# Batch 1's first projections in the ramp, GpSimd as the engine that normalises, three places for rows of q and k, and a new order of the work on every engine

## The reference, cut to what matters

```python
x = layernorm(x + attn(x))        # 32 heads on 8 key/value heads of 8 features, softmax over 256 keys
x = layernorm(x + wkv(x, ctx))    # scan over time: y = (sum of exp(..k) * v) / (sum of exp(..k)), decay w, bonus u
x = layernorm(x + ffn(x))
# ffn: h = square(relu(x @ up_w)) (256 -> 1024); h @ down_w + (x @ expert_weight) * (sum of the top 2 of 8 gate logits)
#      and inside it y is normalised with ln_gamma and ln_beta before the residual is added
def layernorm(x): return (x - mean(x)) / sqrt(var(x) + 1e-5)
```

## Time and profile before

| | |
|---|---|
| median of 3 runs | 216.61 us (215.62 to 217.32) |
| profiled execution: time, span | 216.79 us, 215.0 us |
| TensorE busy | 199.7 us (93%) |
| VectorE busy | 163.1 us (76%) |
| ScalarE busy | 150.9 us (70%) |
| GpSimd busy | 129.6 us (60%) |
| first attention unit, first exponential unit | 13.29 us, 24.80 us |
| exponential unit 64, end of the last unit | 83.65 us, about 169.6 us |
| last matmul | 208.0 us |

### The profile page before, as it was taken

One profiled execution on the slowest core, in us unless ns is written; L12 is line 12 of the kernel. 1 busy time (PEld: TensorE's weight loads), 2 busy tenths in 40 slices (PEclk: granted clock), 3 DMA queues, 4 the chain that ended last, 5 costly groups with the idle time before them and its releaser, 6 DMA issues.

```text
span 215.0 us, 4364 instructions
## 1 busy us (share of the span) xinstructions
PE 199.7 (93%) x1295; PEld 111.7 (52%) x1295; DVE 163.1 (76%) x392; ACT 150.9 (70%) x334; POOL 129.6 (60%) x256
## 2 busy tenths in 40 slices
PE   8889999979999899999999999999999998799970
PEld 3533543433433334575465445664655487698950
DVE  3469778778999899998979899976754837956274
ACT  2310477867899789989799879998967984763520
POOL 8995164753465724567476786867495493177622
PEclk9999999999999999999999999999999999999996
DMA  3145227943116602131000000010000000000001
GB/s 122 43 117 170 70 56 226 255 127 108 27 44 203 218 2 64 49 90 36 19 9 7 2 0 9 2 33 25 2 6 0 3 24 26 2 5 0 24 24 49
DMA packets 14759, 12.35 MB, mean 57 GB/s; under 512 B 3856, under 2 KB 12688, under 8 KB 14480
## 3 DMA queue, kind: packets, MB, share of 16 engines
q1 hardware_dynamic: 14064, 11.72, 19.0%
q10 hardware_dynamic: 672, 0.36, 0.6%
HBM read 6.57 MB, written 1.05 MB: 35 GB/s over the span
## 4 chain that ended last, share of the span: by engine, by line
PE 71%; DMA 8%; DVE 7%; ACT 6%; issue 5%; ACTq 1%; POOL 1%; POOLq 0%; DVEq 0%
PE ps_b L781 10%; PE ps_heads L629 10%; PE ps_exp L613 10%; PE ps_b L764 9%; DMA q_rows<-max_t 7%; PE ps_max L600 6%; PE ps_exp L635 4%; PE ps_exp L764 3%; PE ps_b L747 3%; PE ps_a L722 3%; PE ps_a L676 2%; ACT probs L812 2%; PE ps_a L665 2%; DVE maxima L1180 2%; PE ps_a L585 2%
## 5 line engine op out<-in xcount | busy, mean ns | idle before, releaser
L1180 DVE TENSOR_REDUCE maxima<-ps_max 128x2 f32<-128x512 f32 x128 | 85.0, 684 | 10.6 <-PE ps_max L600 9.7
L812 ACT ACTIVATE probs<-ps_exp 128x512 f32<-128x512 f32 x128 | 73.6, 599 | 14.6 <-PE ps_exp L613 14.1
L613 PE MATMUL ps_exp<-q_rows,k_rows 64*128 64x512 bf16 x128 | 46.2, 385 | 3.8 <-ACT probs L812 1.7
L600 PE MATMUL ps_max<-k_rows,q_rows 64*128 64x256 bf16 x256 | 47.4, 274 | 0.7 <-DMA q_rows<-q_parts 0.6
L613 PEld LDWEIGHTS ps_exp<-q_rows,k_rows 64*128 64x128 bf16 x128 | 11.4, 93 | 45.0 <-ACT probs L812 25.9
L629 PE MATMUL ps_heads<-probs,v_cols 128*32 128x512 f32 x256 | 33.9, 604 | 0.0
L781 PE MATMUL ps_b<-down_sb,inner_t 128*128 128x256 f32 x112 | 29.4, 388 | 0.7 <-ACT relu_t L943 0.7
L764 PE MATMUL ps_b<-x_t,up_sb 128*128 128x128 f32 x192 | 27.1, 285 | 1.1 <-DVE h L1367 1.1
L1061 POOL TENSOR_TENSOR rstd<-var_eps,minus_half 128x1 f32<-128x1 f32 x32 | 19.6, 611 | 11.7 <-DVE var_eps L1154 11.7
L764 PEld LDWEIGHTS ps_b<-x_t,up_sb 128*128 128x128 f32 x192 | 23.2, 191 | 6.0 <-issue 4.0
L781 PEld LDWEIGHTS ps_b<-down_sb,inner_t 128*128 128x128 f32 x112 | 19.4, 190 | 4.3 <-issue 1.5
(11 more groups left out here) (129 smaller groups left out, 345.2 us busy)
## 6 DMA issues: line engine op xcount, KB each, us to landing
q_rows<-q_parts SPq DMA_DIRECT2D x46, 64.0 KB, 2.1
x_t<-in_x_cols SPq DMA_DIRECT2D x4, 256.0 KB, 3.3
x_in<-in_x SPq DMA_DIRECT2D x4, 256.0 KB, 4.5
ctx_t<-in_ctx_cols SPq DMA_DIRECT2D x4, 256.0 KB, 3.0
up_sb<-in_up_w SPq DMA_DIRECT2D x1, 1024.0 KB, 6.1
down_sb<-in_down_w SPq DMA_DIRECT2D x1, 1024.0 KB, 6.1
out_y<-y_out SPq DMA_DIRECT2D x8, 128.0 KB, 1.7
post_sb<-in_w_post SPq DMA_DIRECT2D x1, 906.0 KB, 5.5
```

The costliest lines, as they stand in the source:

```text
L600: last = nc.tensor.matmul(ps_max[n % 2][:, r, :], q_rows[b][at:at + HALF, g, REP * jj + 2 * half + r, h * P:h * P + P], k_rows[b][at:at + ...
L613: nc.tensor.matmul(ps_exp[n % 2][:, :], k_rows[b][at:at + HALF, JH * g + jj, kt * P:kt * P + P], q_rows[b][at:at + HALF, g, REP * jj:REP * ...
L812: nc.scalar.activation(probs[n % 8][:, :], ps_exp[n % 2][:, :], ACT.Exp, scale=SCALE).then_inc(s_exp, 1)
L1180: nc.vector.tensor_reduce(maxima[s % 2][:, g, j // JH, 0, at:at + 2], ps_max[n % 2][:, :, :], AX, ALU.max, negate=True).then_inc(s_max, 1)
```

## The change

1. **Ramp.** Batch 1's x is loaded at the very start. Its k and first q projection (AT 2315 and 2379 before, inside the first units) go to 1618 and 1839, before the first unit. Three idle matmuls follow each of k(1), v(0) and q1(0); the 16 that waited for the rows before the first unit are gone.
2. **Copies of batch 0.** The three copies of k's middle and low part go from ScalarE's queue to GpSimd's, and ScalarE's issues all three copies of group 0's later q parts. Group 0's parts of maxima are made on GpSimd and its `max_t` is evacuated by ScalarE (both VectorE before), v(0) is evacuated by ScalarE, and VectorE fills batch 1's `q_rows`.
3. **Norms.** For p < 6 GpSimd adds epsilon, takes the power and applies mean and rstd (L997 in the new kernel). The negated mean, the offset and ScalarE's part are gone, as is VectorE's addition.
4. **Three places for rows.** `q_rows` and `k_rows` have three tiles instead of four (ROT): batch 3 takes batch 0's, waits until its exponentials are made, and copies zeros over two rows. `probs` has 12 buffers instead of 8.
5. **Order.** Nearly all numbers of AT are new.

```diff
-        "k": (1456, 2315, 2440, 3400),
+        "k": (1474, 1618, 2440, 3368),
-        "q0": (1503, 2379, 2792, 3624),
+        "q0": (1520, 1839, 2762, 3720),
...
+    ROT = 3
+    NPROBS = 12
...
             sp.dma_start(qk_sb[:, KV_COLS:], w_qk[:, KV_COLS:]).then_inc(s_wq, 16)
+            sp.dma_start(flat(x_t[1][:, :, :]), x_cols[1]).then_inc(s_xt[1], 16)
...
+            def rows_free(b):
+                sp.wait_ge(s_ones, ROT + (b >= 2))
+                if b == 1:
+                    sp.wait_ge(s_q1_zero, 1)
+                if b >= ROT:
+                    sp.wait_ge(s_exp, UNITS * TT * (b - ROT + 1))
...
+                                if b >= ROT and qp == 0:
+
+                                    sp.dma_start(row_block(q_rows[b % ROT][:, g], len(BLOCKS)),
+                                                 row_block(q_rows[1][:, g], len(BLOCKS) + 1)).then_inc(s_rows[b][g], 16)
...
-                    if n == 0:
-
-                        for done, value, n_idle in ((s_q2[0], 1, ROW_FILL), (s_q3[0], 1, 6 * ROW_FILL),
-                                                    (s_krows[0], 16 * len(BLOCKS), ROW_FILL)):
-                            pe.wait_ge(done, value)
-                            for k in range(n_idle):
-                                idle_matmul(ident_bf)
...
+                        if b == 1:
+                            for k in range(FILL):
+                                idle_matmul(ident_bf)
...
-                for kp, done in ((1, s_k2), (2, s_k3)):
-                    if AT[f"kc{kp}"][0] == tick:
-                        act.wait_ge(s_ones, 1)
-                        act.wait_ge(done, 1)
-                        k_row_copies(act, 0, kp)
...
+                    if b == 0 and AT["vb"][0] == tick:
+                        act.wait_ge(s_const, 1)
+                        a_filled(act, ("v", 0))
+                        nc.scalar.activation(
+                            heads_of(v_cols[0])[:, :, :, 0:HD],
+                            ps_a[:, 0:TT * KVD].rearrange("p (x j d) -> p x j d", j=GS, d=HD), ACT.Copy).then_inc(s_a_read, 1)
...
+            gp.wait_ge(s_ones, 1)
+            for kp, done in ((1, s_k2), (2, s_k3)):
+                gp.wait_ge(done, 1)
+                k_row_copies(gp, 0, kp, s_krows_pool)
+            gp.memset(q_rows[2][:], 0.0).then_inc(s_ones, 1)
...
+            def normalise(k, p, src, dst, done):
+                gp.wait_ge(s_rstd[k], p + 1)
+                for i in CHUNKS[p][1]:
+                    last = gp.tensor_scalar(dst[:, i, :], src[:, i, :], mean_var[k][:, i, 0:1], rstd[k][:, i:i + 1],
+                                            ALU.subtract, ALU.mult)
+                last.then_inc(done, 1)
...
                             if p < WIDE:
-                                gp.tensor_scalar(neg_mean[k][:, ti], mean_var[k][:, ti, 0], -1.0, None,
-                                                 ALU.mult).then_inc(s_negmean[k], 1)
+                                gp.tensor_scalar(var_eps[k][:, ti], mean_var[k][:, ti, 1], EPS, None,
+                                                 ALU.add).then_inc(s_pool, 1)
+                                npool[0] += 1
+                                gp.wait_ge(s_pool, npool[0])
                             gp.tensor_tensor(rstd[k][:, ti], var_eps[k][:, ti], minus_half[:, ti],
                                              ALU.pow).then_inc(s_rstd[k], 1)
...
+            nc.vector.memset(q_rows[1][:], 0.0).then_inc(s_q1_zero, 1)
```

More of the change, by code:

```diff
@@ new lines, in decoder_layer @@
+        "qc02": (1762, 2656, 3604, 4853),
+        "qc10": (1997, 2958, 3467, 4355),
+        "qc11": (1938, 2853, 3658, 4953),
+        "qc12": (1903, 2941, 3639, 4940),
+        "load": (2173, 2207, 2241, 2578, 2835, 3158, 3326, 3367, 3620, 3709, 4718, 4872, 4979),
[17 rows of a table added]
+        "att": (3181, 3821, 4176, 4700, 5200, 5704, 6125, 6799),
+        "att_e": (3167, 3839, 4217, 4703, 5183, 5661, 6110, 6826),
+        "xbo": (3008, 3038, 3451, 4485, 4864, 5098, 5717, 5824),
[30 rows of a table added]
+        "unit": (4213, 4790, 5355, 5581, 6121, 6242, 6990, 7629),
@@ L275, in decoder_layer @@
         max_t = sb("max_t", [P, NSET, P], bf16)
-        probs = [sb(f"probs{i}", [P, REP * P]) for i in range(8)]
+        probs = [sb(f"probs{i}", [P, REP * P]) for i in range(NPROBS)]
         heads_t = [sb(f"heads_t{i}", [P, REP * P]) for i in range(2)]
@@ L310, in decoder_layer @@
         rstd = [sb(f"rstd{i}", [P, TT]) for i in range(4)]
-        neg_mean = [sb(f"neg_mean{i}", [P, TT]) for i in range(4)]
-        offset = [sb(f"offset{i}", [P, TT]) for i in range(4)]
         ps_max = [ps(f"ps_max{i}", [P, 2, T]) for i in range(2)]
@@ L505, in load @@
             def load(j):
-                tiles = ((x_t[1], x_cols[1], s_xt[1]), (x_in[0], x[0], s_x[0]), (ctx_t[0], ctx_cols[0], s_ctx[0]),
+                tiles = ((x_in[0], x[0], s_x[0]), (ctx_t[0], ctx_cols[0], s_ctx[0]),
                          (x_t[2], x_cols[2], s_xt[2]), (post_sb, w_post, s_w_post), (up_sb, up_w, s_up),
@@ L678, in _ @@
                             last.then_inc(s_q0 if b == 0 else s_a, 1)
+                            if b == 0 and g == 1:
+                                for k in range(FILL):
+                                    idle_matmul(ident_bf)
                     if AT["v"][b] == tick:
@@ L685, in _ @@
                         last.then_inc(s_a, 1)
+                        if b == 0:
+                            for k in range(FILL):
+                                idle_matmul(ident_bf)
                 for s in range(GROUPS):
@@ L791, in evacuate @@
                                      ACT.Copy).then_inc(s_a_read, 1)
-            def affine(dst, src, k, i):
-                return nc.scalar.activation(dst, src, ACT.Identity, scale=rstd[k][:, i:i + 1],
-                                            bias=offset[k][:, i:i + 1])
-            def normalise(k, p, src, dst, done):
-                act.wait_ge(s_offset[k], p + 1)
-                for i in CHUNKS[p][1]:
-                    last = affine(dst[:, i, :], src[:, i, :], k, i)
-                last.then_inc(done, 1)
             act.dma_start(qk_sb[:, 0:KV_COLS], w_qk[:, 0:KV_COLS]).then_inc(s_wkv, 16)
@@ L968, in _ @@
             gp.memset(k_rows[0][:], 1.0).then_inc(s_ones, 1)
-            for i in range(2):
-                gp.memset(maxima[i][:, :, :, PARTS:HD], 0.0).then_inc(s_zeros, 1)
             own(gp.memset(ident[:], 0.0))
@@ L1151, in variance @@
                 for i in tiles:
-                    own(nc.vector.bn_aggr(mean_var[k][:, i, :], stats[k][:, i, :]))
+                    ins = nc.vector.bn_aggr(mean_var[k][:, i, :], stats[k][:, i, :])
+                    if p >= WIDE or i != tiles[-1]:
+                        own(ins)
+                if p < WIDE:
+                    ins.then_inc(s_var[k], 1)
+                    return
                 settle()
@@ L1205, in _ @@
                                                 ALU.add).then_inc(s_a_read, 1)
[L1206 removed]
+                    if b >= 1 and AT["vb"][b] == tick:
                         dve.wait_ge(s_const, b + 1)
```

186 lines of the change are left out of this document (80 added, 106 removed), and 178 rows, old and new, of the table AT.

## The result

The change makes the kernel slower: 220.18 us (median of 4 runs, 219.81 to 220.56) against 216.29 us; ratio 1.0176, 95% interval 1.0129 to 1.0223. The forecast was 213.6 us with a range of 211.0 to 217.5, and 0.13 on slower. The profiled execution has a span of 218.4 us, 3.4 more than before.

A forecast was written before the change was run, and what follows sets the result against it. TensorE was taken as the bound, alone in the second half and with VectorE and ScalarE close behind in the first. Terms -0.6 - 2.3 + 0.9 - 1.2 + 0 + 0.5 - 0.3 = -3.0 gave 213.6 us, range 211.0 to 217.5.

The forecast's parts named there:

- The step that failed: Norms: GpSimd's 128x256 scale and shift was taken at 0.5 us, bounds 0.39 and 0.73, up to 0.91.
- The break-even: Norms: the chain from statistics to x, 1.82 us before and 1.37 after, breaks even at a 0.95 us operation.
- +0.5: Term against the gain: engines hold each other up and the new order has less slack; bounds 0 and +2.5 us.
- Nothing where TensorE bounds: Term for GpSimd's norms: 7.4 us more on GpSimd's 86.5 in 144.8 is not a bound, so 0.
- slower rival: x comes late from GpSimd, behind its products, for twelve TensorE transposes: +4.2, 220.8 us; chance 0.13.
- The sign that I had set for a wrong forecast: TensorE gaps over 1 us between units 64 and 127, or VectorE over 90% busy in the first half.
- Ramp: -0.6: Before the first exponential unit: it starts at 24.2 us instead of 24.80; bounds -1.3 and +1.2.
- Order in the second half: -2.3: Exponential unit 64 to the last: fewer changes between kinds of TensorE work save 2.3 us, unless data come late.
- the group that came in: One group of eight probs x V matmuls moves from the first half to the second: +0.9 there, -0.9 in the first.
- the pair that left: One pair of expert matmuls crosses into the tail from the stage before, taken as 0 net.
- First half: -1.2, bounds 0 and -3: First exponential unit to the 64th: 0.9 us less for the moved group, 0.3 less from gaps.
- Tail: -0.3 + 0.9: After the last exponential: the moved pair adds 0.9 us and partly fills TensorE's waits, -0.3; bounds -0.9 and +0.5.

The follow-up runs named there:

- experiment 1: The changed kernel with the norms of chunks 0 to 5 put back on ScalarE, two slots a few ticks earlier: 220.56 us, ratio 1.0181.
- experiment 6: The changed kernel with GpSimd's scale and shift as multiply and add, the offset in one more 128x1 operation: 216.65 us, ratio 0.9976.
- experiment 7: The changed kernel with VectorE normalising chunks 0 to 5 while GpSimd keeps epsilon and power: 217.04 us, ratio 1.0009.
- experiment 8: The changed kernel with GpSimd's scale and shift as add and multiply, the mean negated on VectorE: 212.93 us, ratio 0.9834.
- experiment 4: The kernel before with GpSimd normalising by subtract and multiply, its old order, ramp and rows kept, one slot two ticks later: 225.09 us, ratio 1.0387.
- experiment 9: The kernel before with GpSimd normalising by add and multiply, in the old order, one slot two ticks later: 217.41 us, ratio 1.0048.
- experiment 2: The changed kernel with GpSimd normalising only 64 of 256 columns, zero fills ahead of its first casts: 217.38 us, ratio 1.0029.

## Why the prediction was wrong

**The step that failed** is the price of the scale and shift on GpSimd: "I take 0.5, bounds 0.39 and 0.73 (up to 0.91 ...)". It measured 1.24 to 1.28 us. I had bounded the price from operations of another kind, a cast and a product, all below the point that I had named as deciding ("it breaks even at 0.95 us"). With the same result made by a form of 0.56 us on the same engine at the same places, the kernel runs in 212.9 us. Of the 7.1 us that separate the two profiled executions, 3.4 are in the second half and 3.3 in the tail.

**The break-even itself was wrong too.** 0.95 us is where the new chain is as long as the old one, 1.82. That is the measure of the old order. In the new order the old chain on ScalarE takes 220.6 (experiment 1), and 0.88 us on GpSimd only equals the kernel before (experiment 6). I had written that "the new order has less slack", that some tiles of x are due sooner, and priced it at **+0.5** with 2.5 at the most. With a norm of 0.56 us that was about its size: the waits left for x from GpSimd are 0.2. With the chains of experiments 6 and 1 the same order takes 3.7 and 7.6 us more (by the medians) than with the cheap one.

**"Nothing where TensorE bounds"** failed with it. The reason given, that GpSimd's load is far from a bound, was true (71.74 of 88.20) and beside the point: each engine's queue is in order, and x has a slot in TensorE's. The **slower rival** had that mechanism, "x comes late from GpSimd", and its 220.8 was close to 220.2, by luck in the detail: I reckoned with twelve transposes late by 0.6 (by my own 0.7 it would have been 222); there were four waits of 3.4 us in all for GpSimd, and two of 3.7 for VectorE, which waited for the power in GpSimd's queue. That path, GpSimd's normalisations of earlier chunks ahead of the power for chunks 6 and 7, stood in no step. The sign that I had set for a wrong forecast did show: TensorE has gaps of more than 1 us between units 64 and 127, the longest 1.7.

**Ramp: -0.6**, measured -0.41 (24.80 to 24.39), with its steps: copy of maxima 21.45 for 21.6, first attention unit 13.58 for 13.9. One execution says no more: five kernels with this same ramp (the changed one, experiments 1, 6, 7 and 8) have F from 23.15 to 24.39, three with the old ramp from 24.50 to 24.80. The mean difference is 0.8, and the term holds. The trace shows GpSimd's copies at 0.60 us each, from 8.55 to 10.35, while VectorE ran subtractions (8.03 to 8.96 and 9.44 to 9.87); its fill of batch 1's rows had ended by 5.27. The warning of the Trainium skill, SBUF — State Buffer, "SBUF: two separate sides", is of VectorE operations that hold the port which the two share, and these subtractions cost the copies nothing here. No run here has such a copy beside a fill or a plain copy of VectorE.

**Order in the second half: -2.3**, measured -1.2: with the norm cheap, H2 went from 85.99 to 84.77, and the group that came in and the pair that left, priced at 0.9 each, cancel. So the direction is right and the size about half. TensorE's busy time fell by 1.9 (85.81 to 83.95), which is nearer to the term, but its idle time rose from 0.2 to 0.8. And this holds only with the short norm: experiment 1 shows the same order at 90.23. What the counts of changes between kinds of work did not tell is that the new order had spent the slack of x for them.

**First half: -1.2, bounds 0 and -3**: -2.6 (58.85 to 56.24), in the changed kernel already. The term was too small by its gaps: 0.3 was taken for them, and they fell by 1.6, from 3.92 to 2.36 us. The engine of the norm is not the reason: with ScalarE normalising in the new order H1 is 56.56 (experiment 1), with GpSimd normalising in the old order 58.91 and 59.01 (experiments 4 and 9). No run separates the new order from the 12 buffers of probs.

**Tail: -0.3 + 0.9** gives 38.6; 39.01 with the cheap norm, 42.27 without.

**What was luck.** With the cheap norm the kernel takes 212.9 us where 213.6 was forecast, but the parts differ: the first half gave 1.5 us more than its term, the order 1.1 less.

**The weighing of the page.** By the Trainium skill, GPSIMD Engine Reference, section 4.1 "Engine selection", an operation with one input is near line rate on GpSimd. VectorE's own operation of this form has a median of 0.41 us in experiment 7. Beside that the traces agree for a copy (0.40) and for multiply and add by constants (0.40), less for pairs without a subtraction (0.55), and not for single steps (0.85 to 0.94) or the form in this change: 1.23, above even the 0.72 of two inputs. The measurement decides.

**Still open.** In experiments 1 and 7 the late x and the fuller queue of the engine that makes it come together. Experiment 6 adds 0.28 us both to the chain and to GpSimd's queue and costs 1.4% (about 3 us, by the two ratios) against experiment 8, which has a negation on VectorE instead. No run lengthens the chain without loading a queue, so their shares aren't known. Why a subtraction makes GpSimd's operation slow, and a single step slower than a pair, is open too.

## What to carry to other kernels

Before moving an operation to another engine, measure that very form there: the same arithmetic, written (x + a) * b instead of (x - c) * b, was 2.2 times as fast on GpSimd, and it decided between +1.8% and -1.7%. Where engines walk fixed queues, ask of a moved operation how late its output may be for the slot of its user, and what else waits in that queue (here a 128x1 power), not whether the engine has time to spare. An order with fewer changes between kinds of TensorE work was worth 1.2 us in 86, and only while its inputs came in time. And a break-even that is worked out in the old order does not hold in a new one that is tighter.

## What the runs showed of the hardware

- GpSimd's tensor_scalar on 128x256 float32: pairs (multiply, add), (add, multiply), (multiply, multiply) by per-partition values 0.55 to 0.56 us; (subtract, multiply) and (multiply, subtract) by such values 1.22 to 1.23, (subtract, multiply) by constants 1.07; (multiply, add) by constants 0.40; a single multiply, add or subtraction 0.85 to 0.94. A pair without a subtraction was faster than one of its steps alone. Each form was timed once or twice by itself; in the kernels (subtract, multiply) took 1.24 to 1.29 on average and (add, multiply) 0.56 to 0.65.
- (Subtract, multiply) by per-partition values costs about 0.37 us and 3.35 ns a column (64 to 512 columns).
- Three DMAs issued by GpSimd took 0.60 us each to write, as on the other queues.
- After TensorE had stood idle for 2.5 us (experiment 4) and 2.8 us (experiment 2), the granted clock was 0.50 for about 3.3 us. In experiment 4 work of 2.36 us took 3.93 in that stretch.
